# Fused attention and quantised FFN: the output projection of two pairs at once in every second round, shared row buffers, reordered score tiles and shorter idle products

## The reference, cut to what matters

```python
xn = layernorm(x)
q, k, v = split_heads(xn @ Wq), split_heads(xn @ Wk), split_heads(xn @ Wv)
w = softmax(q @ k.T / 64 + causal)             # per head, 1024 x 1024
w = w * clip((key_no + span * 1024) / 33, 0, 1)
w = w / (sum(w) + 1e-8)
attn = merge_heads(w @ v) @ Wo                  # Wo: 1024 x 128
ffn = (clip(round(xn / s), -127, 127) * s) @ (ternary - 1).T + bias
out = x + attn + ffn
```

## Time and profile before

| | us |
|---|---|
| median of 3 runs | 1015.55 |
| lowest and highest | 1015.36 and 1018.13 |
| the profiled execution's own time | 1013.19 |
| its span in the trace | 1011.5 |

### The profile page before, as it was taken

How to read it: one execution, slowest core, us unless ns; L and a number is a source line. 1 busy time by engine, 2 the same in 40 slices (tenths; PEclk the granted TensorE clock), 3 DMA queues, 4 the chain that set the end, 5 groups by cost and what they waited for, 6 DMA issues and landing times.

```text
span 1011.5 us, 19162 instructions
## 1 busy us (share of the span) xinstructions
PE 987.6 (98%) x7087; PEld 626.0 (62%) x7087; DVE 766.3 (76%) x1734; ACT 455.0 (45%) x607; POOL 708.9 (70%) x650
## 2 busy tenths in 40 slices
PE   7899999999999999999999999999999999999998
PEld 3565665666665666666666666666666666665654
DVE  8778788878788888877767877777877777777752
ACT  4344454444454444454444454444454444454442
POOL 8576767678766668767767677667766667767673
PEclk9999999999999999999999999999999999999999
DMA  6000000000000000000000000000000000000000
GB/s 174 3 3 2 2 2 2 2 2 3 2 22 2 3 2 3 1 3 2 3 12 12 2 3 2 2 3 2 2 2 24 2 3 2 1 2 2 2 1 22
DMA packets 16117, 8.52 MB, mean 8 GB/s; under 512 B 5388, under 2 KB 15628, under 8 KB 16024
## 3 DMA queue, kind: packets, MB, share of 16 engines
q1 hardware_dynamic: 15416, 7.16, 2.7%
q10 hardware_dynamic: 608, 0.14, 0.1%
HBM read 4.33 MB, written 2.10 MB: 6 GB/s over the span
## 4 chain that ended last, share of the span: by engine, by line
PE 84%; DVE 11%; issue 3%; DMA 1%; ACT 1%; SPq 0%; DVEq 0%; ACTq 0%
PE pv L956 25%; PE ring L939 24%; PE ring L912 12%; PE beside L995 7%; PE beside L968 6%; DVE v L718 3%; PE ring L885 3%; PE ring L881 3%; PE ring L882 3%; DVE ring L732 2%; DVE beside L756 2%; PE pv L1001 1%; PE beside L983 1%; PE beside L919 1%; DVE rowmax L732 1%
## 5 line engine op out<-in xcount | busy, mean ns | idle before, releaser
L541 ACT ACTIVATE prob<-ring 128x1024 f32<-128x1024 f32 (+3 forms) x384 | 294.3, 812 | 352.1 <-PE ring L939 337.1
L475 POOL TENSOR_TENSOR psumd<-psumd,prob 128x512 f32<-128x512 f32 (+1 forms) x252 | 410.5, 1629 | 28.3 <-POOL psumd L475 0.4
L732 DVE CUSTOM_DVE_ANT_0 ring<-ring,causal 128x128 f32<-128x128 f32 (+3 forms) x512 | 240.4, 516 | 98.0 <-PE ring L912 97.4
L939 PE MATMUL ring<-q,k 64*128 64x512 f32 (+3 forms) x2304 | 279.1, 348 | 3.6 <-DMA mrow<-maxrow 2.4
L956 PE MATMUL pv<-prob,v 128*64 128x512 f32 (+3 forms) x1536 | 267.2, 490 | 0.0
L448 POOL TENSOR_SCALAR_AFFINE_SELECT prob<-prob 128x256 f32<-128x256 f32 x256 | 107.0, 419 | 207.4 <-ACT prob L541 205.2
L939 PEld LDWEIGHTS ring<-q,k 64*128 64x128 f32 x2304 | 192.5, 185 | 39.1 <-DVE rowmax L732 5.2
L956 PEld LDWEIGHTS pv<-prob,v 128*64 128x64 f32 x1536 | 104.7, 137 | 153.6 <-issue 141.9
L471 POOL TENSOR_TENSOR psumd<-prob 128x768 f32<-128x768 f32 x64 | 135.2, 2112 | 43.3 <-ACT prob L541 38.6
L736 DVE TENSOR_REDUCE rowmax<-ring 128x2 f32<-128x1024 f32 x128 | 153.7, 1222 | 13.6 <-PE ring L912 10.3
L912 PE MATMUL ring<-k,q 64*128 64x512 f32 (+3 forms) x768 | 143.2, 409 | 8.7 <-DVE v L718 6.2
(11 more groups left out here) (112 smaller groups left out, 945.6 us busy)
## 6 DMA issues: line engine op xcount, KB each, us to landing
x_sb<-in_L_attn_query SPq DMA_DIRECT2D x4, 512.0 KB, 5.4
kext<-kext SPq DMA_DIRECT2D x128, 4.0 KB, 1.7
out<-x_sb SPq DMA_DIRECT2D x8, 256.0 KB, 2.3
mrow<-maxrow SPq DMA_DIRECT2D x64, 4.0 KB
xn_sb<-in_L_attn_Wv SPq DMA_DIRECT2D x1, 512.0 KB, 5.6
wo<-in_L_attn_Wo SPq DMA_DIRECT2D x1, 512.0 KB, 7.2
xn_sb<-in_L_attn_Wq SPq DMA_DIRECT2D x1, 448.0 KB, 3.4
xn_sb<-in_L_attn_Wk SPq DMA_DIRECT2D x1, 448.0 KB, 4.1
```

Source lines behind the costliest of these rows:

```text
L475: g.tensor_tensor(acc[:, :, lo:HALF], acc[:, :, lo:HALF], pr[:, :, lo:HALF], ALU.add).then_inc(acc_done, 1)
L541: a.activation(prob[n % NPROB][:, :, lo:HALF], ring[:, slot(f"S{t}", i), :, lo:HALF], ACT.Exp, scale=1.0 / DH).then_inc(exp_done, 1)
L732: last = v.tensor_tensor_reduce(out=ring[:, s, h, 0:n], in0=ring[:, s, h, 0:n], in1=causal[:, HALF - n:HALF], scale=1.0, scalar=MASKED, op ...
L939: last = t_.matmul(ring[:, s, h, lo:HALF], k[p][rows, keys], q[p][rows, cols], start=(at == 0), stop=(at == len(parts) - 1))
```

## The change

- **Output projection.** Y happens only for odd pairs. It multiplies the halves of pairs i-1 and i with their parts of Wo and sums both in PSUM: 16 instructions in place of 8 in each Y, 16 groups for each half in place of 32. Y1 thus stands in even rounds only (it is written "Y1-") and Y0 in odd rounds only. The normalised halves have four buffers (`o_sb`), and VectorE's addition (Ya) is there as often as Y.
- **TensorE's plan.** S3 goes ahead of V; S5 ahead of M4; S7 ahead of M6 and M7, directly behind Y1; S11 ahead of M10 and M11, directly behind Y0.
- **VectorE's plan.** u1 goes ahead of Vs, o1 ahead of R4, R8 ahead of u0, and R11 ahead of Ya0.
- **GpSimd's plan.** A0 and A1 go behind later L's, and A7 moves from before L8 to behind L9; A8 stands between L9 and L10.
- **Opening.** 6 idle products of 256 columns in place of 9 of 512 columns, between M2 and M8 alone. The first six, ahead of everything, stay at 512.
- **Memory.** The normalised rows have two buffers in turn in place of one for the whole input; the raw weights land in `prob` buffers, so the first exponential waits for the splitting of the weights. The third batch's normalisation moves from rounds 11 and 12 to 16 and 17, and the third addition of the bias from round 14 to 18.

The diff:

```diff
--- before.py
+++ after.py
@@ -33,14 +33,15 @@
 
 
 
-PE_PLAN = ("T Q+ K+ X0 X1 W G11- M0+ M1+ S0 S1 S2 M2+ D1- M3+ V+ S3 S4 M4+ S5 S6 M5+ Y1- M6+ M7+ S7 D0 G3 "
-           "M8+ S8 S9 S10 M9+ Y0 M10+ M11+ S11 G7")
+
+PE_PLAN = ("T Q+ K+ X0 X1 W G11- M0+ M1+ S0 S1 S2 M2+ D1- M3+ S3 V+ S4 S5 M4+ S6 M5+ Y1- S7 M6+ M7+ D0 G3 "
+           "M8+ S8 S9 S10 M9+ Y0 S11 M10+ M11+ G7")
 ACT_PLAN = "Z Qhi+ Khi+ X0 X1 E0 E1 E2 ln1- ex1- E3 E4 E5 E6 E7 ln0 ex0 E8 E9 E10 E11"
-DVE_PLAN = ("Tc Z Qlo+ Klo+ R0+ R1+ X0 X1 W R2+ R3+ t1- Vs+ u1- R4+ o1- R5+ Ya1- R6+ R7+ t0 u0 R8+ o0 q "
-            "R9+ R10+ Ya0 R11+ Rc+")
-POOL_PLAN = "L0 A0 L1 A1 L2 A2 L3 A3 A4 A5 A6 A7 L8 L9 L10 L11 A8 A9 A10 A11 B"
-
-PE_FIRST = ("Q+ K+ M0+ M1+ M2+ I0+ M3+ I1+ M4+ I2+ M5+ I3+ M6+ I4+ M7+ I5+ M8+ I6+ M9+ I7+ M10+ I8+ M11+ Q++ T+ "
+DVE_PLAN = ("Tc Z Qlo+ Klo+ R0+ R1+ X0 X1 W R2+ R3+ t1- u1- Vs+ o1- R4+ R5+ Ya1- R6+ R7+ t0 R8+ u0 o0 q "
+            "R9+ R10+ R11+ Ya0 Rc+")
+POOL_PLAN = "L0 L1 A0 L2 L3 A1 A2 A3 A4 A5 A6 L8 L9 A7 A8 L10 L11 A9 A10 A11 B"
+
+PE_FIRST = ("Q+ K+ M0+ M1+ M2+ I0+ M3+ I1+ M4+ I2+ M5+ I3+ M6+ I4+ M7+ I5+ M8+ M9+ M10+ M11+ Q++ T+ "
             "K++ S0+ S1+ S2+ V+")
 DVE_FIRST = ("Qlo+ Klo+ R0+ R1+ R2+ R3+ R4+ R5+ R6+ R7+ R8+ R9+ R10+ R11+ Rc+ Tc+ Qlo++ Klo++ keys+ Vs+")
 ACT_FIRST = "xf0+ Qhi+ xf1+ Khi+ rest+ keys+ wv+ Qhi++ Khi++ E0+ E1+ E2+"
@@ -60,7 +61,7 @@
 
 
 STEP_OF = {1: "stats1", 2: "var1+", 3: "norm1a", 4: "norm1b", 5: "stats2", 6: "stats3", 7: "var2",
-           8: "rstd2", 9: "norm2a", 10: "norm2b", 11: "norm3a", 12: "norm3b"}
+           8: "rstd2", 9: "norm2a", 10: "norm2b", 16: "norm3a", 17: "norm3b"}
 
 
 def happens(name, i):
@@ -73,12 +74,14 @@
         return i == LAST
     if name[0] == "I":
         return i == 0
+    if name[0] == "Y":
+        return i % 2 == 1
     if name == "q":
         return i % PAIRS_OF_BATCH < PAIRS_OF_BATCH - 1
     if name == "Z":
         return i in STEP_OF
     if name == "B":
-        return i in (6, 11, 14)
+        return i in (6, 11, 18)
     if name == "store":
         return i % PAIRS_OF_BATCH == PAIRS_OF_BATCH - 1
     return True
@@ -145,14 +148,11 @@
             return ctx.enter_context(nc.semaphore(name))
 
         x_sb = sb("x_sb", [P, NB, D])
-        xn_sb = sb("xn_sb", [P, NB * P])
+        xn_sb = [sb(f"xn{n}", [P, S]) for n in range(2)]
         x1 = [sb(f"x1_{n}", [P, S], F32R) for n in range(2)]
         x2 = [sb(f"x2_{n}", [P, S], F32R) for n in range(2)]
         xf = sb("xf", [P, S])
         fq = sb("fq", [P, S])
-
-        w_raw = [xn_sb[:, (B - 2 + n) * S:(B - 1 + n) * S] for n in range(2)]
-        wv_raw = xn_sb[:, S:2 * S]
         w1 = [sb(f"w1_{n}", [P, H * DH], F32R) for n in range(2)]
         w2 = [sb(f"w2_{n}", [P, H * DH], F32R) for n in range(2)]
         wv1 = sb("wv1", [P, H * DH], F32R)
@@ -173,13 +173,16 @@
         v_sb = [sb(f"v_{p}", [P, KB, 4, DH]) for p in range(2)]
         NPROB = 8
         prob = [sb(f"prob_{n}", [P, 2, HALF]) for n in range(NPROB)]
+
+        w_raw = [prob[n][:, :, :].rearrange("p c n -> p (c n)") for n in range(2)]
+        wv_raw = prob[2][:, :, :].rearrange("p c n -> p (c n)")
         psumd = [sb(f"psumd_{c}", [P, 2, HALF]) for c in range(2)]
 
         minus_one, plus_one = psumd[0][0:1, :, :], psumd[1][0:3, :, :]
         lnden = sb("lnden", [P, HALF])
         r0 = sb("r0", [P, HALF])
         rden = sb("rden", [P, HALF])
-        o_sb = [sb(f"o_{c}", [P, HALF]) for c in range(2)]
+        o_sb = [[sb(f"o_{p}_{c}", [P, HALF]) for c in range(2)] for p in range(2)]
         rowmax = [sb(f"rowmax{p}", [P, P]) for p in range(2)]
         rowmax2 = [sb(f"rowmax2_{p}", [P, 2, HB]) for p in range(2)]
         maxrow = sb("maxrow", [2 * KB, P], F32R)
@@ -286,6 +289,9 @@
         def slot(name, i):
             return PLACE[name, i] % NSLOT
 
+        def outputs_upto(i, c):
+            return halves_upto(i // 2, c)
+
         def den_bank(i, c):
 
             return ring[:, slot("D1", i), 0, :] if ("D1", i) in PLACE and c == 1 else beside[:, :]
@@ -362,9 +368,9 @@
                     place_key_weights(i, i % 2)
                 else:
                     b = i // NPB
-                    sp.wait_ge(y_added, halves_upto(i, 0))
+                    sp.wait_ge(y_added, outputs_upto(i, 0))
                     store(b, 0, HB)
-                    sp.wait_ge(y_added, halves_upto(i, 1))
+                    sp.wait_ge(y_added, outputs_upto(i, 1))
                     store(b, HB, KB)
             sp.wait_ge(out_stored, 16 * 2 * B)
 
@@ -481,7 +487,7 @@
                 elif name[0] == "A":
                     add(i, int(name[1:]))
                 else:
-                    add_bias((6, 11, 14).index(i) + 1)
+                    add_bias((6, 11, 18).index(i) + 1)
 
         @block.scalar
         def _(act):
@@ -535,6 +541,9 @@
                 lo = first_col(t)
                 n = i * NT + t
                 act.wait_ge(scores_ready, tiles_upto(i, t))
+                if n == 0:
+                    act.wait_ge(w_lo_done, 4)
+                    act.wait_ge(wv_lo_done, 1)
                 if n >= NPROB:
                     act.wait_ge(pv_done, n - NPROB + 1)
                     act.wait_ge(acc_done, n - NPROB + 1)
@@ -627,7 +636,7 @@
 
             def normalise(b, n0, n1):
                 for n in range(b * KB + n0, b * KB + n1):
-                    v.tensor_scalar(xn_sb[:, n * P:(n + 1) * P], x_sb[:, n, :], mv[:, n, 0:1],
+                    v.tensor_scalar(xn_sb[b % 2][:, (n - b * KB) * P:(n - b * KB + 1) * P], x_sb[:, n, :], mv[:, n, 0:1],
                                     rstd[:, n:n + 1], ALU.subtract, ALU.mult).then_inc(xn_done, 1)
 
             def turned(b, c, src):
@@ -653,7 +662,7 @@
 
             def quantise(b, step):
 
-                over = xn_sb[:, b * S:(b + 1) * S].bitcast(U32)
+                over = xn_sb[b % 2][:, :].bitcast(U32)
                 if b or step > 1:
                     dve.wait_ge(fq_step, b * FQ_STEPS + (step - 1))
                 else:
@@ -687,11 +696,11 @@
                 elif step == "rstd2":
                     rstd_finish(3, slice(2 * KB, NB))
                 else:
-                    if step == "norm1a":
-                        dve.wait_ge(w_lo_done, 4)
-                        dve.wait_ge(wv_lo_done, 1)
+                    b = int(step[4])
+                    if b > 1:
+                        dve.wait_ge(turned_ready, 2 * (b - 2) + 2)
                     n0 = HB * "ab".index(step[5])
-                    normalise(int(step[4]), n0, n0 + HB)
+                    normalise(b, n0, n0 + HB)
 
             def key_weights():
 
@@ -765,13 +774,15 @@
 
                 dve.wait_ge(rden_done, halves_upto(i, c))
                 dve.wait_ge(pv_done, tiles_upto(i, HB - 1 if c == 0 else NT - 1))
-                v.scalar_tensor_tensor(out=o_sb[c][:, :], in0=pv[:, :], scalar=-1.0, in1=rden[:, :],
+                if i >= 2:
+                    dve.wait_ge(y_ready, outputs_upto(i - 2, c))
+                v.scalar_tensor_tensor(out=o_sb[i % 2][c][:, :], in0=pv[:, :], scalar=-1.0, in1=rden[:, :],
                                        op0=ALU.mult, op1=ALU.mult).then_inc(o_done, 1)
 
             def add_output(i, c):
 
                 b = i // NPB
-                dve.wait_ge(y_ready, halves_upto(i, c))
+                dve.wait_ge(y_ready, outputs_upto(i, c))
                 dve.wait_ge(bias_added, b + 1)
                 rows = x_sb[:, b * KB + c * HB:b * KB + (c + 1) * HB, :]
                 v.tensor_tensor(rows, rows, beside[:, :].rearrange("p (n d) -> p n d", n=HB),
@@ -852,7 +863,7 @@
                 elif unit[0] == "D":
                     pe.wait_ge(rden_done, halves_upto(j, int(unit[1:])))
                 elif unit[0] == "Y":
-                    pe.wait_ge(y_added, halves_upto(j, int(unit[1:])))
+                    pe.wait_ge(y_added, outputs_upto(j, int(unit[1:])))
                 elif unit[0] == "X":
                     pe.wait_ge(x2_done, 2 * batch_of_turn(j) + int(unit[1:]) + 1)
                 else:
@@ -862,8 +873,8 @@
 
                 pe.wait_ge(xn_done, b * KB + (c + 1) * HB)
                 for k in range(HB):
-                    n = b * KB + c * HB + k
-                    last = t_.transpose(out[:, k * P:(k + 1) * P], xn_sb[:, n * P:(n + 1) * P], ident[:, :])
+                    n = c * HB + k
+                    last = t_.transpose(out[:, k * P:(k + 1) * P], xn_sb[b % 2][:, n * P:(n + 1) * P], ident[:, :])
                 last.then_inc(turned_ready, 1)
 
             def projection(i, name):
@@ -986,23 +997,25 @@
             def output_projection(i, c):
 
                 with_ffn = i % NPB == NPB - 1
-                if i == 0 and c == 0:
+                if i == 1 and c == 0:
                     pe.wait_ge(wo_landed, 16)
                 if with_ffn and (f"F{c}", i) not in PLACE_BESIDE:
                     feed_forward(i, c)
                 pe.wait_ge(o_done, halves_upto(i, c))
                 for k in range(HB):
```

(16 more changed lines are left out.)

## The result

The changed kernel takes 1036.26 us (median of 4 runs, 1034.69 to 1039.47), the kernel before 1015.45 (4 runs). The ratio is 1.020, interval 1.017 to 1.023: slower by 20.8 us. The profiled execution took 1034.69 us with a span of 1033.0; against the profiled one of before the span grew by 21.5.

The account below looks back on a forecast made before the run. TensorE, busy for 98% of the span, was taken as the bound. Opening -2.6, even rounds 7 x 0.94 and 8 x 1.2, odd rounds 15 x 0.03 and 3 x 0.75, last round +1.0: +17.3 on 1013.2, so 1030 us; range 1008 to 1040.

Parts of the forecast that it names:

- The hidden wait at the end of the round: Even rounds' end: VectorE's combining of the maxima is held until GpSimd's A8 ends, so T comes 0.55 us later.
- q and the select of tile 8: Even rounds' tail: VectorE's later quantisation step holds GpSimd's select; with a plain step +0.94 us per round, +0.69 without holding.
- The coin that I split: Even rounds with a predicated step: the combining goes before A8, +0.81 us, or behind, +1.56; the middle, +1.2, was taken.
- TensorE's own work: TensorE per round: pairing's savings go to slot waits; +0.14 us in even rounds, +0.03 in odd ones.
- Rounds 7, 15 and 23: Odd rounds whose Y0 also carries the feed-forward: the combining falls inside GpSimd's A9, +0.75 us each.
- the moved normalisation: Normalisation moved to other rounds: counted among the edits at nothing.
- The opening: Before T of pair 0: shorter idle products let VectorE's maxima follow without idling, gain 2.6 us, from 0 to 2.6.
- Rival 4: Opening: shorter idle products lose the granted clock, costing 3 us more and giving 1033; chance 0.1 beside any case.
- rival 1: Even rounds' end: the combining gets through before A8 starts, giving 1014 us; chance 0.13.
- rival 2: M4 and R4's slot: TensorE's waits shrink, some -0.6 us per two rounds, with the opening 1003; chance 0.18.
- rival 3: Odd rounds' end: the combining slips behind A9 in part of them, 1.8 us, giving 1040 or more; chance 0.06.
- The value unit's part: Around V and M4, every round: M4 still waits 0.2 us, one score tile more is done, S6 onward 0.22 earlier.

Follow-up runs that it names:

- run 1: Changed kernel with the maxima combined by a reduce over one SBUF operand in place of an elementwise maximum of two: 1022.1 us.
- run 2: Changed kernel with GpSimd's A7 ahead of L8 again: 1020.9 us.
- Run 5: Changed kernel with u0 ahead of R8 again, so that the quantisation step q starts earlier: 1029.7 us.
- run 10: Changed kernel with A7 ahead of L8, u0 ahead of R8 and the maxima combined over one operand: 1013.8 us, ratio 0.997.
- run 4: Changed kernel's projection of two pairs, shared row buffers and moved normalisation, with the kernel before's engine plans, opening and long idle products: 1035.2 us.
- run 8: Kernel before with the six shorter idle products and nothing else: 1012.9 us, ratio 0.998.
- run 9: Changed kernel with the nine long idle products of the kernel before: 1040.7 us.
- run 7: Kernel before with S3 ahead of V, S5 ahead of M4 and o1 ahead of R4, Vs still ahead of u1: 1005.2 us, ratio 0.990.
- run 11: Kernel before with run 7's order, the six short idle products and the maxima combined over one operand: 1002.6 us, ratio 0.986.
- run 6: Kernel before with S3 ahead of V, S5 ahead of M4, u1 ahead of Vs and o1 ahead of R4: 1007.6 us, ratio 0.992.

## Why the prediction was right

- **The hidden wait at the end of the round.** The prediction read that Rc is held by GpSimd's addition and that 0.26 us covered it. Counted from the exponential of tile 9, it put A8's end at +5.31 and T 0.55 behind TensorE, 0.80 with a plain q; in round 18 it is 0.74. Round 18 shows T at 30.85 us for a forecast 30.89, S8 at 22.32 for 22.35. Runs 1 and 2 take the wait away from two sides and win the same. By the Trainium skill's "SBUF — State Buffer", section "Who interferes with whom", a VectorE instruction with two SBUF inputs and a GpSimd one that reads SBUF exclude each other for their whole length, and a `tensor_reduce` never contends; this case agrees: 1.82 and 2.32 us for the pair of inputs, 0.17 for the reduce.
- **q and the select of tile 8.** Right in kind for both sorts of step: with a plain q of 0.74 beside it the first of the two selects at 617.18 takes 0.87 us, and one that nothing holds takes 0.41. So +0.94 for the round was the value to take and not +0.69; the seven rounds measure 0.89 on average. The Trainium skill's "SBUF — State Buffer", section "Who interferes with whom", has `tensor_scalar` among the instructions that can hold GpSimd off, and this trace agrees. Run 5 shows what q's late place costs: 0.65 in rounds with a predicated step, and 0.1 in the others, less than the 0.25 that I had for a plain one.
- **The coin that I split.** Rc and A8 were 0.04 apart in rounds with a predicated step, and I took the middle, +1.2. Rc went behind in all eight (2.32 us), +1.5 each. This term was 2.2 too small. Of two ends 0.75 apart one had to come true in every round alike, and a middle between them could only be wrong; the order in the trace (A8 at 184.81, Rc at 184.85) was that of my two figures, A8 first.
- **TensorE's own work.** +0.14 and +0.03 for even and odd rounds; with the rest removed (run 10) they are 30.12 and 29.90, against 29.95: +0.17 and -0.05. (The working's -1.1 for no slot waits is -1.03 by its own terms; nothing hangs on it.) Slots that are waited for eat what the pairing saves, and run 4 says so without the other edits. Both new waits are where I put them: S11 0.31 at 617.86, and S7 in odd rounds behind R4:

```profile
639.22 0.97 PE L950 MATMUL ring<-q,k 64*128 64x512 f32 x6 [0.27 <-DVE rowmax L745]
```

- **Rounds 7, 15 and 23:** +0.76, +0.62 and +1.13 for 0.75. Why round 23 lost 0.4 more than the others is open; it does so in run 1 too, where Rc is free.
- **What was missing: the normalisation rounds.** I put the moved normalisation at nothing. Rounds 3, 9 and 17 are 0.7, 0.4 and 1.0 longer. In round 17, VectorE's four normalisation instructions and GpSimd's A9 to A11 start together:

```profile
562.18 3.75 DVE L639 TENSOR_SCALAR xn<-x_sb,mv,rstd 128x128 f32<-128x128 f32 x4
```

```profile
562.15 4.38 POOL L481 TENSOR_TENSOR psumd<-psumd,prob 128x768 f32<-128x768 f32 x3
```

  The four take 1.94, 0.33, 1.37 and 0.33 us; the long two end 0.07 and 0.08 behind an addition, so GpSimd holds these `tensor_scalar` instructions too. Before, the first took 1.21 in round 17's place, round 12. Run 2, in which A7 and with it A9 are early, has these three rounds at 29.9, and run 1, in which they are late but Rc is free, at 30.3. So A7's place costs here too. With round 11, which is 0.7 shorter since its normalisation has left it, these make up the 1.4 of the twelve odd rounds.
- **The opening.** The gain was 1.6 at T of pair 0 and not 2.6, and the prediction missed its own mechanism here. VectorE was through with the maxima 3.3 earlier (Rc is issued at 30.04, for 33.33 before), more than the 2.6; but there Rc now meets GpSimd's addition of the bias, which before was over at 31.75:

```profile
30.04 1.91 DVE L752 TENSOR_TENSOR rowmax<-rowmax,rowmax 128x8 f32<-128x8 f32 x1
```

```profile
29.58 2.35 POOL L444 TENSOR_TENSOR x_sb<-x_sb,bias_b 128x1024 f32<-128x1024 f32 x1
```

  Rc took 1.91 there for 0.17, and T of pair 0, at 32.01, came right behind it. Run 10, where Rc is a reduce, has T at 30.8.
- **Rival 4, the clock,** came true beside the forecast, but not at its price of 3 us. The row of the changed kernel in that stretch (columns as in run 8):

```profile
28.00:35.00 7.00, 5.38 (x13) 3.27 (x12) 5.32 (x11) 1.02 (x1) 3.92 (x2) 0.51 0.02 4
```

  The granted clock, 0.51, is near the lower of its two levels, 1.2 GHz for 2.4, and the projection products go from start to start in 0.43 for 0.23. It seems to have cost about 0.4: T of pair 0 was held by Rc in any case, and round 0 is 30.53 for 30.17 in run 9, where the clock was full there. The rival's reason (more rest with short products) fits the runs: in the stretch before, from 18 to 28, TensorE was busy for 8.20 us, for 9.78 in the kernel before; and between 28 and 33 the granted clock is 0.50 to 0.71 in all seven profiles with short products and 1.00 in all six with long ones. The fall in run 9 is an earlier one, of which both kinds have examples: with long products (runs 7 and 9) it was over by 27.0, with short ones (runs 1, 2 and 11) a fall that began near 20 lasted until 34.7 to 36.9.
- **Rivals 1, 2 and 3** did not come; Rc takes 0.16 in the twelve other odd rounds. The value unit's part does hold what rival 2 asked for, 0.3 per round (run 6); the sum had only 0.2 of it, since the earlier Y1 was counted in the pairing.
- **Luck and misses.** In the opening two errors made up for each other in part: 3.3 won on VectorE for 2.6, and 1.7 lost in Rc unseen. Of the sum the predicated rounds lack 2.2, the opening with round 0 1.3 and the odd rounds 1.2, and the plain even rounds and the end are 0.5 too high; so nearly all misses point one way, and the time came in the upper part of the range.

## What to carry to other kernels

When a unit is taken out of the engine that bounds, look what was waited for behind it: here Y had hidden the release of two PSUM slots, and with A7's move the end of one tiny VectorE instruction as well, and taking it out turned all three into waits. Two engines that hold each other off meet in the plans, not in the totals: an instruction of 0.17 us took up to 2.3 because one of 2.4 stood ahead of it. Make it a reduce over one SBUF operand (run 1), or move the long one out of its way (run 2). When a hold of this kind is found in one place, look for it at every place where a change makes the two engines meet: here also in the opening and in the rounds with normalisation. Test the parts of a bundle alone: one of these parts was worth -8 us under a sum of +21.

## What the hardware showed that was not expected

The granted clock in the opening differs from run to run of the same kernel: the changed kernel's mean clock was 0.996, 0.988, 0.995 and 0.995 in four runs, for 1034.7, 1039.5, 1036.2 and 1036.3 us. T of pair 0 came at 33.6 to 38.6 us with nine long idle products (six profiles) and at 30.8 to 35.4 with six short ones (seven profiles). The fall between 28 and 33 us goes with the short ones, as said above, and part of T's place is Rc's hold. A fall before 28 us is found with both (runs 7 and 9; runs 1, 2, 5, 8 and 11), and what decides it stays open. So differences of 2 to 3 us between whole times of this kernel should be read from the rounds instead.
